# Attention probabilities: VectorE divides both heads of pair 1, GpSimd none of them

## The chip, the cores and the metric

The kernel runs on one core of a Trainium2 chip. Its five engines are TensorE (PE; its weight loads are shown apart as PEld), VectorE (DVE), ScalarE (ACT), GpSimd (POOL) and SyncE (SP), which issues the DMAs. The metric is the time of one execution on the device in microseconds, lower is better. Each engine runs its own program in order; they wait for each other on semaphores.

## What is computed

The reference takes x and a context of shape (4, 1024, 512) and does two things, all in fp32:

```python
x = x + banded_attention(layernorm(x), ctx, ctx)      # band of 128, one head of 512
x = x + two_layers(layernorm(x))
# each layer, HEADS = 8, DIM_HEAD = 64, WINDOW = 256:
q, k, v = split(shift_token(x) @ wqkv)
q, k = rotary_xpos(l2norm(q) * q_scale, l2norm(k) * k_scale)
sim = where(i < j or i > j + 256, -big, 8 * q @ k.T)
x = x + (softmax(sim) @ v) @ wo
h = layernorm(shift_token(x)) @ w1 + b1
a, g = split(h)
x = x + (a * gelu(g)) @ w2 + b2
```

What matters here is softmax(sim) @ v of the two layers: exponentials, their sums, and the division by the sums before the product with v.

## The kernel before

The 4096 rows are 32 tiles of 128. The program is a banded stage, then for each of two layers an attention stage (attend) and an FFN stage (ffn). Products in fp32 precision are made from a high and a low half of each operand: ScalarE makes the high half by a rounding copy (copy, L1363), VectorE the low half by a subtraction (low, L1727), and TensorE multiplies three combinations.

In attend(l), step s works on tile t = s - 2 for scores and probabilities while it projects tile s and rotates tile s - 1. k = t % 8 is the place of a tile in its sequence; it sees 1, 2 or 3 key tiles (k = 0, 1, from 2 on), so rows of probabilities are 128, 256 or 384 columns wide. The eight heads are four pairs; a pair's probabilities stand in one buffer lprob of 128 x 2 x 384. Each step has two halves, d = 0 for pairs 0 and 1, d = 1 for pairs 2 and 3. For a half of a tile:

- TensorE: scores(t, d) (L1094), two pairs after each other. Before its second pair it waits for hT_low, the low half of the transposed input: of tile s at d = 0, of tile s + 1 at d = 1. In this step VectorE makes the half of tile s + 1, in hT (split_h).
- VectorE: maximum(t, h) for the four heads of the half (L1893; it adds the mask, writes the exponents to lprob and gives the least value; a small read of an accumulator follows).
- ScalarE: probabilities (L1542), the exponentials with their sums.
- VectorE: divide(t, p) takes the reciprocals of a pair's two sums (L1878) and multiplies. Pair 0 is done whole by VectorE with one tensor_tensor (L1883). Of pairs 1, 2 and 3 (LATE_PAIRS) VectorE does the second head with a tensor_scalar (L1881) and GpSimd the first with another (divide in pool_program, L2295).
- TensorE: turn_probabilities (L1116) half a step later, pair 1 before pair 0; it waits for the maxima of the whole tile (lmax), since it writes the banks of the scores, and for each head's division (wait_scaled). ScalarE copies the result (lprobT), and mix (L1133) multiplies it with v.

VectorE's order at d = 0 is: four maxima, rope(.., 0) (with_cos and with_sin, L1917), norm_sum (L1825), divide(t, 0), divide(t, 1), rope(.., 1), split_h, then split_parts (even t, 2 to 22) or split_sums (odd t, 1 to 21), low halves of FFN weights that are prepared on the side. At d = 1 it begins with the next four maxima and split_out, divides pairs 2 and 3, and ends with split_q and split_k.

GpSimd's order in a step is: in some steps sums of weight parts (sum_parts), rotate(.., 0) (L2304), inverse_norm (a clamp, L2221, and a power function, L2222), divide(t, 1), scale_rotated(.., 0) (L2315), rotate(.., 1), scale_rotated(.., 1), divide(t, 2), divide(t, 3). What scale_rotated leaves in turned_qk is transposed by TensorE in turn_q and turn_k (L897) at the end of the step. The order on every engine is written out by hand in the loops over s.

Of the kernel before, what the change touches and what calls it, by code (L numbers as in the profile page):

```python
# [60 lines left out]
def hid_rows(j):  # L61
    return min(P, HID - j * P)
# [63 lines left out]
def reach(t):  # L126
    k = t % TPB
    w = min(k, 2) + 1
    return k, w, w * P, (k - w + 1) * P
# [5 lines left out]


PAIRS = HEADS // 2
LATE_PAIRS = (1, 2, 3)


PARTS = (2, 0, 1)
# [33 lines left out]
def early_tile(s):  # L175

    i, odd = divmod(s - NORMALISE_AT, 2)
    return i if 0 <= i < GROUP and not odd else None


def prepared_item(s, after):

    item, odd = divmod(s - PREPARE_AT - after, 2)
    return item if 0 <= item < HC and not odd else None


def summed_rows(s, after):

    pair = s - PREPARE_AT - 2 * HC - after
    return pair if pair in (0, 1) else None  # L190
# [24 lines left out]
def build(nc, x, ctx, mask, wqkv, q_scale, k_scale, wo, ln_g, ln_b, w1, b1, w2, b2, consts, out):  # L215
# [266 lines left out]
    def rotated_tile(s):  # L482

        return 0 if s == 0 else s - 1 if 2 <= s <= TILES else None

    def rotated_by_gpsimd(l, t, part):

        return 4 * (l * TILES + t) + 2 * (part + 1) - 2 * (l + ((t, part) > (0, 0)))
# [403 lines left out]
    def tensor_program(e):  # L892
# [146 lines left out]
        def attend(l):  # L1039
# [59 lines left out]
            def wait_scaled(n, p, i):  # L1099
                if p not in LATE_PAIRS:  # L1100
                    w.wait_ge(S("pscaled"), PAIRS * n + p + 1)
                elif i:
                    w.wait_ge(S("pscaled"), PAIRS * n + p + 1)
                else:
                    w.wait_ge(S("pscaled_pool"), len(LATE_PAIRS) * n + LATE_PAIRS.index(p) + 1)

# [610 lines left out]
    def vector_program(e):  # L1717
# [145 lines left out]
        def attend(l):  # L1863
# [8 lines left out]
            def divide(t, p):  # L1872
# [6 lines left out]
                w.wait_ge(S("rden"), PAIRS * n + p + 1)  # L1879
                if p in LATE_PAIRS:  # L1880
                    ins = e.tensor_scalar(prob[:, 1, 0:cols], prob[:, 1, 0:cols], inverse[:, 1:2], None, ALU.mult)  # L1881
# [280 lines left out]
    def pool_program(e):  # L2162
# [3 lines left out]
        def settle(ins):  # L2166

            ins.then_inc(S("pool_settled"), 1)
            w.wait_ge(S("pool_settled"), next(settled))
# [40 lines left out]
        def scale_tables(l):  # L2210
            A = attends[l]
            w.wait_ge(S("rope_in"), 64 * (l + 1))
            spread = A.scales[:, :].unsqueeze(1).to_broadcast([P, TPB, 2 * HD])
            for table in (A.rope_cos, A.rope_sin):
                e.tensor_tensor(table[:, :, :], table[:, :, :], spread, ALU.mult).then_inc(S("rope_scaled"), 1)

        def inverse_norm(l, t):
            n = l * TILES + t
            nm = norm[:, n % 2, :]
            w.wait_ge(S("norm_sum"), n + 1)  # L2220
            settle(e.tensor_scalar(nm[:, 0:16], nm[:, 0:16], NORM_FLOOR ** 2, 0.0, ALU.max, ALU.add))  # L2221
            e.tensor_tensor(nm[:, 16:32], nm[:, 0:16], half_power[:, :], ALU.pow).then_inc(S("norm_inverse"), 1)  # L2222
# [31 lines left out]
        def attend(l):  # L2254
            A, base = attends[l], l * TILES

            def wait_phase():

                if l:
                    w.wait_ge(S("down"), GROUP * GROUPS * HC * l)  # L2260
                    w.wait_ge(S("f_out"), base)
                else:
                    w.wait_ge(S("mix"), TILES)
                    w.wait_ge(S("x1"), TILES)

            def combine(op, to, a, b):
                return e.tensor_tensor(to, a, b, op)

            def sum_parts(j):

                n = 2 * hid_rows(j)
                g1, a1, a2, g2 = (raw_sum[:, i * n:(i + 1) * n] for i in range(4))
                s1, s2, s3, s4 = (part_sum[:, i * n:(i + 1) * n] for i in range(4))
                w.wait_ge(S("parts_in"), 48 * (l * (HC + 2) + j + 1))
                settle(combine(ALU.add, s1, g1, g2))
                combine(ALU.subtract, s3, a1, g1)
                settle(combine(ALU.subtract, s2, s1, a1))
                combine(ALU.subtract, s4, a2, s2).then_inc(S("part_sums"), 1)

            def sum_first_rows(pair):  # L2280

                odd1, even1, even2, odd2 = (raw_sum[:, i * HALF:(i + 1) * HALF] for i in range(4))
                t1, t2, t3, t4 = (part_sum[:, i * HALF:(i + 1) * HALF] for i in range(4))
                w.wait_ge(S("parts_in"), 48 * (l * (HC + 2) + HC + pair + 1))
                settle(combine(ALU.subtract, t1, odd1, even1))
                combine(ALU.subtract, t3, odd2, odd1)
                settle(combine(ALU.subtract, t2, odd2, t1))
                combine(ALU.subtract, t4, even2, t2).then_inc(S("part_sums"), 1)

            def divide(t, p):  # L2290

                n, cols, sm = base + t, reach(t)[2], small[:, (base + t) % 2, :]
                prob = A.prob[p][:, 0, 0:cols]
                w.wait_ge(S("rden"), PAIRS * n + p + 1)
                e.tensor_scalar(prob, prob, sm[:, 16 + 2 * p:17 + 2 * p], None, ALU.mult).then_inc(S("pscaled_pool"), 1)  # L2295

            def rotate(t, part):
                n, h2 = base + t, HD // 2
                turned, cos, sin = (by_head(x[:, part, :]) for x in (A.turned_qk, A.with_cos, A.with_sin))
                w.wait_ge(S("with_cos"), 2 * n + part + 1)  # L2300
                w.wait_ge(S("with_sin"), 2 * n + part + 1)
                w.wait_ge(S("k_turned") if part else S("q_turned"), n)
                for a, b in ((0, h2), (h2, 0)):
                    e.tensor_tensor(turned[:, :, a:a + h2], cos[:, :, a:a + h2], sin[:, :, b:b + h2],  # L2304
                                    ALU.add).then_inc(S("rotated"), 1)

            def scale_rotated(t, part):
                n = base + t
                turned = by_head(A.turned_qk[:, part, :])
                inverse = norm[:, n % 2, 16 + part * HEADS:16 + (part + 1) * HEADS]  # L2310
                w.wait_ge(S("rotated"), rotated_by_gpsimd(l, t, part))
                if part and t == 0:
                    w.wait_ge(S("first_rotated"), 2 * (l + 1))
                w.wait_ge(S("norm_inverse"), n + 1)
                e.tensor_tensor(turned, turned, inverse.unsqueeze(2).to_broadcast([P, HEADS, HD]),  # L2315
                                ALU.mult).then_inc(S("qk_scaled"), 1)

            if l:
                scale_tables(l)
            wait_phase()  # L2320
            for s in range(TILES + 3):
                t = s - 2
                live, rotating = 0 <= t < TILES, rotated_tile(s)
                if l and s == 0:
                    inverse_norm(l, 0)
                if prepared_item(s, 1) is not None:
                    sum_parts(prepared_item(s, 1))
                if summed_rows(s, 1) is not None:
                    sum_first_rows(summed_rows(s, 1))
                if s == 2:  # L2330
                    inverse_norm(l, 1)
                if rotating is not None:
                    rotate(rotating, 0)
                if rotating and s > 2:
                    inverse_norm(l, rotating)
                if live:
                    divide(t, 1)
                if rotating is not None:
                    scale_rotated(rotating, 0)
                    if rotating:  # L2340
                        rotate(rotating, 1)
                    scale_rotated(rotating, 1)
                if early_tile(s) is not None:
                    inverse_deviation(l, early_tile(s))
                if live:
                    divide(t, 2)
                    divide(t, 3)

        def inverse_deviation(l, t):
            reciprocal_deviation(stats[:, t % 2, :], "ln", l * TILES + t).then_inc(S("ln_rstd"), 1)  # L2350
# [40 lines left out]
        for l in range(DEPTH):  # L2391
            attend(l)
            ffn(l)
# [58 lines left out]
```

## Time and profile before

| | |
|---|---|
| time, median of 3 runs | 2882.64 us (2881.0 to 2884.29) |
| time of the profiled execution | 2882.62 us |
| its span | 2880.8 us |
| busy: PE, PEld | 2863.6, 2521.9 us |
| busy: DVE, ACT, POOL | 2069.0, 1346.0, 1308.8 us |
| TensorE's granted clock | 1.00 |

The busy times are of the whole span and average over stages with different limits. The ends of matmuls are modelled, so a gap of TensorE that is short can show as a longer group of matmuls, or as a gap between two weight loads, and not as idle time. In a window, the columns are its ends and length, then for PE, PEld, DVE, ACT and POOL the busy us (and instructions), then the granted clock, the DMA engines' share and GB/s. In the timeline a row is start, duration, engine, line, operation, output<-inputs, shapes and count of instructions merged; in brackets the idle time before it and what ended it. Instructions of one engine overlap by some 0.08 us from row to row. A power function of GpSimd works on 16 columns only.

### The profile page before, as it was taken

To read this page: it belongs to the slowest core of one execution; us is meant where nothing else is said; L and a number is where in the kernel's file an instruction comes from. 1 tells how busy PE (TensorE), PEld (TensorE's weight loads), DVE (VectorE), ACT (ScalarE), POOL (GpSimd) and SP (SyncE) were. 2 spreads that over 40 slices of the span, in tenths; PEclk is the share of its full clock that TensorE was granted. 3 is DMA by queue.
4 is the path that set the end of the run, shared out by engine and by line. 5 is a ranking of instruction groups with operands and counts; after the bars stand their busy time and mean duration, and the time that the engine had idled before them with its cause. 6 is when DMAs were issued, how large, how long until landed. Compare 5 with 4: busy or idle time off the path is not lost. (4 is left out here: it accounts for less than half of the span.)

```text
span 2880.8 us, 53016 instructions
## 1 busy us (share of the span) xinstructions
PE 2863.6 (99%) x20256; PEld 2521.9 (88%) x20256; DVE 2069.0 (72%) x4135; ACT 1346.0 (47%) x2807; POOL 1308.8 (45%) x1406
## 2 busy tenths in 40 slices
PE   9999999999999999999999999999999999999999
PEld 7887888888889999999998888888888999999998
DVE  8987677776677666766657777776677776676765
ACT  7875556565564222222235566655555322223221
POOL 7857676776641211122105676776662223222221
PEclk9999999999999999999999999999999999999999
DMA  6753233322047777777783223332127777777775
GB/s 218 237 187 109 94 109 103 121 92 81 30 178 299 271 273 265 269 265 258 262 312 120 96 94 108 111 118 90 51 66 294 278 276 272 274 288 281 282 268 195
DMA packets 184897, 547.02 MB, mean 190 GB/s; under 512 B 26678, under 2 KB 82490, under 8 KB 162116
## 3 DMA queue, kind: packets, MB, share of 16 engines
q1 hardware_dynamic: 184500, 543.57, 53.0%
q8 instruction: 161, 2.64, 0.4%
q14 instruction: 92, 0.75, 0.1%
q10 hardware_dynamic: 144, 0.07, 0.0%
HBM read 447.11 MB, written 93.70 MB: 188 GB/s over the span
## 5 line engine op out<-in xcount | busy, mean ns | idle before, releaser
L1251 PE MATMUL quad<-fhT_f,slot_f 128*128 128x256 f32 (+1 forms) x2088 | 594.6, 285 | 0.0
L1252 PE MATMUL quad<-fhT_f,slot_f 128*128 128x256 f32 (+1 forms) x2088 | 590.0, 283 | 0.0
L1253 PE MATMUL quad<-fhT_f,slot_f 128*128 128x256 f32 (+1 forms) x2088 | 589.9, 283 | 0.0
L1253 PEld LDWEIGHTS quad<-fhT_f,slot_f 128*128 128x128 f32 (+1 forms) x2088 | 392.7, 188 | 0.0
L1252 PEld LDWEIGHTS quad<-fhT_f,slot_f 128*128 128x128 f32 (+1 forms) x2088 | 392.7, 188 | 0.0
L1251 PEld LDWEIGHTS quad<-fhT_f,slot_f 128*128 128x128 f32 (+1 forms) x2088 | 392.5, 188 | 0.0
L1674 ACT ACTIVATE gate_f_raw<-gate_f_raw,bias_f 128x512 f32<-128x512 f32 (+1 forms) x176 | 127.2, 723 | 551.1 <-DVE gate_f_raw L2097 551.1
L1542 ACT ACTIVATE lprob<-lprob,small 128x384 f32<-128x384 f32 (+2 forms) x512 | 288.7, 566 | 138.5 <-DVE small L1893 138.5
L2187 POOL TENSOR_SCALAR stats<-stats 128x1 f32<-128x1 f32 x64 | 35.4, 553 | 690.1 <-DVE stats L2037 689.3
L2304 POOL TENSOR_TENSOR turned_qk<-with_cos,with_sin 128x256 f32<-128x256 f32 x252 | 183.1, 747 | 334.3 <-DVE with_sin L1917 242.4
L1000 PE MATMUL bank_pair<-wqkv_h,hT 128*128 128x512 f32 x992 | 323.6, 407 | 0.0
L1893 DVE CUSTOM_DVE_ANT_0 lprob<-quad,far 128x384 f32<-128x384 f32 (+2 forms) x512 | 229.2, 503 | 99.5 <-PE quad L1094 99.2
L2295 POOL TENSOR_SCALAR lprob<-lprob,small 128x384 f32<-128x384 f32 (+2 forms) x192 | 226.4, 1186 | 18.4 <-DVE small L1878 18.4
L1363 ACT ACTIVATE lprobT<-quad 128x768 f32<-128x768 f32 (+2 forms) x256 | 173.1, 728 | 103.2 <-PE quad L1116 103.0
L2363 POOL TENSOR_TENSOR res_f<-res_f,bias_f 128x512 f32<-128x512 f32 x63 | 87.8, 1394 | 283.0 <-DMA res_f<-stream 283.0
L2108 DVE SCALAR_TENSOR_TENSOR u_f<-sums_f,bias_f,gate_f_raw 128x512 f32<-128x512 f32 (+1 forms) x176 | 148.1, 841 | 93.3 <-ACT gate_f_raw L1674 93.3
L1000 PE MATMUL bank_pair<-wqkv_l,hT 128*128 128x512 f32 x496 | 201.7, 407 | 0.0
L2222 POOL TENSOR_TENSOR norm<-norm,half_power 128x16 f32<-128x16 f32 x64 | 195.9, 3061 | 5.3
L1000 PEld LDWEIGHTS bank_pair<-wqkv_h,hT 128*128 128x128 f32 x992 | 173.3, 189 | 25.5
L1727 DVE TENSOR_TENSOR qT<-quad,qT 128x512 fp32r<-128x512 f32 x64 | 44.3, 691 | 203.5 <-ACT qT L1363 203.5
L1133 PEld LDWEIGHTS bank<-lprobT,v_rows 128*64 128x64 f32 x2688 | 144.1, 137 | 45.3 <-issue 42.0
L2097 DVE TENSOR_TENSOR gate_f_raw<-quad,sums_f 128x512 f32<-128x512 f32 (+1 forms) x174 | 120.3, 691 | 79.9 <-PE quad L1253 77.1
(296 smaller groups left out, 7469.1 us busy)
## 6 DMA issues: line engine op xcount, KB each, us to landing
slot_f<-parts SPq DMA_DIRECT2D x160, 1792.0 KB, 7.5
slot_f<-parts SPq DMA_DIRECT2D x16, 1190.0 KB, 5.2
s_in<-stream SPq DMA_DIRECT2D x128, 128.0 KB, 2.8
s_res<-stream SPq DMA_DIRECT2D x64, 256.0 KB, 2.9
stream<-a_out SPq DMA_DIRECT2D x64, 256.0 KB, 2.0
res_f<-stream SPq DMA_DIRECT2D x63, 256.0 KB, 7.2
h_in_f<-stream SPq DMA_DIRECT2D x112, 128.0 KB, 6.7
parts<-part_high SPq DMA_DIRECT2D x20, 512.0 KB, 2.6
```

The lines of the kernel that those rows point to most:

```text
L1000: ins = e.matmul(bank, A.hT[n % 2][:, i % 2, c * P:(c + 1) * P], (wqkv_l if i == 2 else wqkv_h)[:, c, cols], start=(c, i) == (0, 0), stop= ...
L1133: ins = e.matmul(banks[5][half, p * P:(p + 1) * P], A.v_rows[:, k - tiles + 1 + j, h * HD:(h + 1) * HD], A.probT[p % 2][:, i, j * P:(j + 1 ...
L1251: e.matmul(bank[0:n, :], high, row_high, start=c == 0, stop=False)
L1252: e.matmul(bank[0:n, :], high, row_low, start=False, stop=False)
L1253: ins = e.matmul(bank[0:n, :], low, row_high, start=False, stop=c == 1)
L1363: return e.activation(to, source, ACT.Copy)
L1542: e.activation(prob, prob, ACT.Exp, bias=sm[:, h:h + 1], scale=-1.0, accum_out=sm[:, 8 + h:9 + h]).then_inc(S("lprob"), 1)
L1893: e.tensor_tensor_reduce(A.prob[h // 2][:, h % 2, 0:cols], quad[:, pair_banks(h // 2) + h % 2, 0:cols], A.far[:, WIN - cols:], 1.0, BIG, A ...
L2108: e.scalar_tensor_tensor(out=Fm.u[q % 2][0:n, :], in0=flat(Fm.sums[q % 2][0:n, 0:2, :]), scalar=Fm.bias1[0:n, 0, j:j + 1], in1=Fm.gate[q % ...
L2222: e.tensor_tensor(nm[:, 16:32], nm[:, 0:16], half_power[:, :], ALU.pow).then_inc(S("norm_inverse"), 1)
L2295: e.tensor_scalar(prob, prob, sm[:, 16 + 2 * p:17 + 2 * p], None, ALU.mult).then_inc(S("pscaled_pool"), 1)
L2304: e.tensor_tensor(turned[:, :, a:a + h2], cos[:, :, a:a + h2], sin[:, :, b:b + h2], ALU.add).then_inc(S("rotated"), 1)
```

## The change

The tuple of pairs that are divided by both engines loses pair 1, and GpSimd's call for it goes:

```diff
-LATE_PAIRS = (1, 2, 3)
+LATE_PAIRS = (2, 3)
@@ pool_program, attend @@
                 if rotating and s > 2:
                     inverse_norm(l, rotating)
-                if live:
-                    divide(t, 1)
                 if rotating is not None:
                     scale_rotated(rotating, 0)
```

The tuple is read in two more places. In VectorE's divide, pair 1 now takes the branch of pair 0: one tensor_tensor over both heads, with the two reciprocals as a broadcast operand. In TensorE's wait_scaled, both heads of pair 1 wait for pscaled, VectorE's count, and the count of GpSimd, pscaled_pool, goes up by two a tile, not three. No other instruction is added, removed or moved.

## Rows read from the trace of the kernel before

**Rows 1.** The page: busy time, then one window; columns as under the table above

```profile
PE 2863.6 (99%) x20256; PEld 2521.9 (88%) x20256; DVE 2069.0 (72%) x4135; ACT 1346.0 (47%) x2807; POOL 1308.8 (45%) x1406
...
250.00:800.00 550.00, 550.00 (x4050) 451.76 (x4049) 401.31 (x971) 325.99 (x736) 376.38 (x357) 1.00 0.27 91
```

**Rows 2.** Groups by line and form, VectorE, then GpSimd: count | busy us, mean ns

```profile
L1883 DVE TENSOR_TENSOR lprob<-lprob,small 128x768 f32<-128x768 f32 x48 | 54.4, 1133 | 1.7
L1883 DVE TENSOR_TENSOR lprob<-lprob,small 128x512 f32<-128x512 f32 x8 | 7.0, 880 | 0.3
...
L2295 POOL TENSOR_SCALAR lprob<-lprob,small 128x384 f32<-128x384 f32 x144 | 187.6, 1310 | 18.4 <-DVE small L1878 18.4
```

**Rows 3.** Whole run, waits of TensorE and its weight loads: us, times, longest

```profile
PE quad L897 <- POOL turned_qk L2315: 1.8, 3, 0.6
PE quad L1116 <- DVE small L1893: 0.5, 2, 0.2
...
PEld quad L1094 <- DVE hT L1727: 0.5, 2, 0.2
```

**Rows 4.** Timeline, tile 0 of layer 0 (k = 0): start us, duration us, engine, line

```profile
224.27 2.93 POOL L2222 TENSOR_TENSOR norm<-norm,half_power 128x16 f32<-128x16 f32 x1
225.12 0.42 DVE L1883 TENSOR_TENSOR lprob<-lprob,small 128x256 f32<-128x256 f32 x1
225.66 0.29 DVE L1881 TENSOR_SCALAR lprob<-lprob,small 128x128 f32<-128x128 f32 x1
...
227.79 0.41 PEld L1094 LDWEIGHTS quad<-kT,qT 64*128 64x128 f32 x6 [0.23 <-DVE hT L1727]
```

**Rows 5.** Timeline, tile 9 of layer 0 (k = 1): TensorE and VectorE

```profile
395.12 0.98 PE L1094 MATMUL quad<-kT,qT 64*128 64x256 f32 x12
...
400.67 0.35 DVE L1881 TENSOR_SCALAR lprob<-lprob,small 128x256 f32<-128x256 f32 x1
...
402.13 0.68 DVE L1727 TENSOR_TENSOR hT<-quad,hT 128x512 fp32r<-128x512 f32 x1
...
402.33 1.16 PE L1094 MATMUL quad<-kT,qT 64*128 64x256 f32 x12
```

**Rows 6.** Timeline, tile 10 of layer 0 (k = 2)

```profile
419.36 0.42 DVE L1881 TENSOR_SCALAR lprob<-lprob,small 128x384 f32<-128x384 f32 x1
419.48 3.09 POOL L2222 TENSOR_TENSOR norm<-norm,half_power 128x16 f32<-128x16 f32 x1
...
420.89 0.68 DVE L1727 TENSOR_TENSOR hT<-quad,hT 128x512 fp32r<-128x512 f32 x1
...
421.68 0.19 PEld L1094 LDWEIGHTS quad<-kT,qT 64*128 64x128 f32 x2
```

**Rows 7.** Timeline, tile 13 of layer 0 (k = 5)

```profile
482.47 0.69 DVE L1727 TENSOR_TENSOR hT<-quad,hT 128x512 fp32r<-128x512 f32 x1
...
484.11 0.19 PEld L1094 LDWEIGHTS quad<-kT,qT 64*128 64x128 f32 x2
...
485.99 0.55 DVE L1893 CUSTOM_DVE_ANT_0 lprob<-quad,far 128x384 f32<-128x384 f32 x1
...
487.08 1.46 PEld L1116 LDWEIGHTS quad<-ident,lprob 128*128 128x128 f32 x12
...
487.31 1.47 PE L1116 MATMUL quad<-ident,lprob 128*128 128x128 f32 x12
```

**Rows 8.** Timeline, last two tiles of layer 0 (30 and 31)

```profile
821.78 1.25 POOL L2295 TENSOR_SCALAR lprob<-lprob,small 128x384 f32<-128x384 f32 x1
...
823.35 1.53 PE L1116 MATMUL quad<-ident,lprob 128*128 128x128 f32 x12 [0.23 <-DVE small L1893]
...
826.78 0.66 PE L897 MATMUL quad<-ident,turned_qk 128*128 128x128 f32 x4 [0.60 <-POOL turned_qk L2315]
...
833.72 0.96 DVE L1883 TENSOR_TENSOR lprob<-lprob,small 128x768 f32<-128x768 f32 x1
...
834.85 1.47 POOL L2295 TENSOR_SCALAR lprob<-lprob,small 128x384 f32<-128x384 f32 x1 [5.67 <-DVE small L1878]
```

## The prediction

> **What bounds the kernel now.** I read the page's busy times first, then windows over the stages, then the waits of TensorE, then the timeline tile by tile. TensorE is busy for 99% of the span, and in a window of 550 us inside the first attention stage for all of it, at full granted clock; VectorE is busy for 401 of its 550 us and GpSimd for 376 [rows 1]. So neither VectorE nor GpSimd is the bound there. TensorE runs a fixed list of work for each tile, and the others only have to be in time for each of its waits. The waits that the profile books to TensorE are few: 1.8 us in three places for GpSimd's rotated queries and keys, 0.5 us in two for a maximum, and 0.5 us of its weight loads for the hT halves [rows 3]. That sets the most that can be won: little over 2 us of 2883. The question is therefore not how much work moves, but whether VectorE, given more to do inside a tile, becomes late for a wait of TensorE.
>
> In a tile VectorE's order is: four maxima of the first scores, the rope of queries, the squared norm, the division of pair 0, the division of pair 1, the rope of keys, the low half of hT, in most tiles a low half of the FFN weights, then the four maxima of the second scores. From the division of pair 0 to the hT half it runs without a gap, except where k = 0. TensorE needs two things from that string: hT, before the second half of scores(t, 1) (the wait on hT_low at an odd pair), and the last maximum, before turn_probabilities(t, 0).
>
> **What the change costs VectorE.** It removes one tensor_scalar over one head and puts a tensor_tensor over both in its place, 64 times. The old one takes 0.29, 0.35 and 0.42 us at 128, 256 and 384 columns [rows 4 to 6]. For the new one there are two prices in the rows of pair 0. Where GpSimd is idle, or sits in its power function, 2x128 columns took 0.42 and 2x384 took 0.96 [rows 4, 8]; between these, 2x256 is (0.42 + 0.96)/2 = 0.69. Where GpSimd's own tensor work stands beside it, the means are 0.88 at 2x256 and 1.13 at 2x384 [rows 2], 0.19 and 0.17 more. Which holds for pair 1? Its slot begins at 419.36, and GpSimd enters the 3.09 us power function at 419.48 [rows 6]; that is the situation of tile 0, where the pair 0 division of 0.42 ran inside the power function [rows 4]. I take the lower price: 0.13 more at 128 columns, 0.34 at 256, 0.54 at 384. The upper one gives about 0.32, 0.53 and 0.72.
>
> **Where it reaches TensorE.**
> - k = 1 (8 tiles, 4 a layer). The hT half ends at 402.13 + 0.68 = 402.81, 0.48 after scores(9, 1) began. That group already takes 1.16 against 0.98 for the same twelve matmuls before it [rows 5]: it stands still for some 0.18 already, so the slack is nothing and all of the 0.34 arrives. 8 x 0.34 = 2.7 us.
> - k = 2 (8 tiles). hT ends at 420.89 + 0.68 = 421.57; the first weight load behind the wait is at 421.68 [rows 6]. A release takes about 0.05 (227.79 in [rows 4] follows an hT half that ended at 227.74), so 0.06 is left, say 0.05. 0.54 - 0.05 = 0.49 arrives. 8 x 0.49 = 3.9 us.
> - k = 0. In the first tile of a layer the loads already sat still 0.23 for hT [rows 4]: 2 x 0.13 = 0.3 us. In the later ones VectorE idles before hT, and the addition is hidden.
> - k = 3 to 7. hT ends at 483.16 and is wanted at 484.11 [rows 7]: 0.95 less 0.05 covers 0.54. The last maximum ends at 485.99 + 0.55 = 486.54, and the loads of the turning begin at 487.08 [rows 7]: 0.49 after the release. The addition passes that by 0.05, but the load runs 0.23 ahead of its matmul (487.31), which takes up the rest: nothing, at this price. At 0.72 the load would be 0.23 late, of which that lead takes up between none and all; the middle, 0.12, would come through in the 16 tiles with odd k from 3 on that also split weight sums. Tiles with even k have VectorE idle before those maxima.
> - Stalls add up. Between two tiles VectorE idles for a microsecond or more waiting for the queries' high half, so it is in time again for the next, and TensorE has no idle time left in which to make one good.
>
> **What GpSimd gives back.** It loses 64 divisions, 1.31 us for the wide ones [rows 2], some 75 to 80 us of its own time. TensorE sees only the ends. In tile 30 GpSimd divides pair 1 at 821.78 for 1.25 us ahead of scaling and rotating tile 31, and TensorE then stands 0.60 us for the keys at 826.78 [rows 8]. Without the division GpSimd is done about 0.7 us sooner (1.25 less the 0.54 by which its power function, queued behind the longer division for their common port, starts later). But TensorE also arrives later: at 823.35 it already waits 0.23 for a maximum [rows 8], so 0.54 goes straight in there. 0.54 - 0.60 = -0.06, twice: -0.1 us. The remaining wait on GpSimd stands before layer 1's first tile, where nothing has been divided yet. The FFN stages have none of these instructions.
>
> **Sum.** 2.7 + 3.9 + 0.3 - 0.1 = 6.8 us. The profiled execution took 2882.62 us around its span of 2880.8, the median of the three runs is 2882.64: the same. 2882.6 + 6.8 = 2889.4 us, 0.24% slower. A measurement of this kernel tells about 0.2%, 5.8 us, from no change, so the forecast lies just beyond that.
>
> **The port rule.** In tile 0 the 0.42 us division ran wholly inside GpSimd's 2.93 us power function, which reads and writes SBUF [rows 4]; it was not held. The Trainium skill ("SBUF — State Buffer", Who interferes with whom) says that a VectorE instruction with two SBUF inputs and a GpSimd instruction that reads SBUF exclude each other for the whole instruction, whoever starts first. By that rule the 0.42 us division would have waited for the function's end, and the new one would wait whenever GpSimd gets in first; the row speaks against it for this function.
>
> **Rivals.**
> - Contended price. If GpSimd's work does stand beside the new division, as beside pair 0 [rows 2]: 8 x 0.53 + 8 x 0.67 + 2 x 0.32 + 16 x 0.12 + 2 x (0.72 - 0.60) = 12.4 us, 2895.0. For it: the norm's small clamp has only just ended when the division starts. Against it: the tensor_scalar in that slot shows its short 0.42.
> - Not slower: the cover holds. One mechanism: the pair 0 division loses its 0.19, because GpSimd, now early, does its clamp elsewhere, and hT comes nearly as before. k = 1 then keeps 0.15 and k = 2 keeps 0.30: 8 x 0.15 + 8 x 0.30 = +3.6, 2886.2, no measurable change. Were also the rest covered, only GpSimd's two waits of 0.60 would go: 2881.4. It decides where VectorE's string up to hT grows by less than 0.3 us a tile. Against it: GpSimd's rotation waits for VectorE's rope itself, so it cannot come earlier.
> - Power function first. If GpSimd enters it before the division and holds the port throughout, the division waits up to 3.09 us [rows 6]: hT late by 0.54 + 3.09 - 0.05 = 3.6 at k = 2, and the maxima by 3.1 beyond their slack in the others. 60 x 3 = 180 us, 3063. The order (419.36 before 419.48) and [rows 4] speak against it. This is what the port rule would give once the order flips; the Trainium skill's page named above states that rule.
>
> **How the numbers follow.** Chances: the forecast 0.56, contended price 0.18, cover holds 0.23 (0.10 at 2886, 0.13 at 2881), power function first 0.03. The forecast's own spread is 2886.5 to 2892: 0.15 us either way in each of the 16 tiles with k = 1 and 2. A quarter of it lies below the bound. So slower 0.42 + 0.18 + 0.03 = 0.63; same 0.14 + 0.20 = 0.34; faster, if GpSimd's relief shortens VectorE's own operations as well, 0.03. The range leaves out the 3063, most of the 0.13 and the top of the contended case: 2883.5 to 2896.5.
>
> **What the profile of the changed kernel would show.** Right: L1883 x128, with pair 1's near 0.96, 0.69 and 0.42; L1881 x128; L2295 x128; weight loads of L1094 waiting for hT in some 18 places, about 7 us in all; the tiles with k = 1 and 2 longer by 0.3 and 0.5 us, the rest unchanged; the 0.60 at the ends of both attention stages gone. Wrong if pair 1's division takes 1.1 or more, if k = 3 to 7 grow, or if scores(t, 1) at k = 2 still runs in one piece.

## The result and the profile after

The changed kernel takes 2888.63 us (median of 11 runs, 2887.63 to 2889.64) against 2882.51 us for the kernel before (11 runs): 6.1 us more, a ratio of 1.0021 with a 95% interval of 1.0013 to 1.0029. The prediction was 2889.4 us, with a range of 2883.5 to 2896.5.

The page's busy line and the window of [rows 1], now of the kernel after:

```profile
PE 2866.8 (99%) x20256; PEld 2522.6 (87%) x20256; DVE 2095.2 (73%) x4135; ACT 1345.8 (47%) x2807; POOL 1261.7 (44%) x1342
...
250.00:800.00 550.00, 548.63 (x4033) 449.22 (x4032) 408.09 (x963) 323.62 (x729) 355.75 (x327) 1.00 0.27 91
```

VectorE has 7 us more to do in this window and GpSimd 21 less. TensorE, which had no idle time in it, now has 1.4 us that the profile shows. Groups by line and form, as [rows 2]:

```profile
L1883 DVE TENSOR_TENSOR lprob<-lprob,small 128x768 f32<-128x768 f32 x96 | 100.3, 1045 | 3.3
...
L1883 DVE TENSOR_TENSOR lprob<-lprob,small 128x512 f32<-128x512 f32 x16 | 12.6, 787 | 0.6
...
L2295 POOL TENSOR_SCALAR lprob<-lprob,small 128x384 f32<-128x384 f32 x96 | 123.8, 1299 | 22.3 <-DVE small L1878 22.3
...
L2222 POOL TENSOR_TENSOR norm<-norm,half_power 128x16 f32<-128x16 f32 x64 | 224.4, 3507 | 5.3
```

The new division of pair 1 is averaged with pair 0's: (2 x 1045 - 1133) is 957 ns at 2x384 columns, (2 x 787 - 880) is 694 ns at 2x256. Pair 1's own instances bear that out: 0.96 us from k = 2 on, 0.69 at k = 1, 0.43 at k = 0, and none of the 64 takes longer than that. GpSimd's power function, which took 3.06 us on average, takes 3.51. It begins 0.11 us after the division, and at k = 1 it grew from 3.02 to 3.37, from k = 2 on from 3.09 to 3.63: by 0.35 and 0.54, as much as the division did. Waits of TensorE, then of its weight loads, as [rows 3]:

```profile
PE quad L897 <- POOL turned_qk L2315: 0.6, 1, 0.6
...
PE quad L1116 <- DVE small L1893: 0.5, 2, 0.3
```

```profile
PEld quad L1094 <- DVE hT L1727: 8.2, 18, 0.5
```

The weight loads of the scores stood twice for hT, 0.5 us; now 18 times, 8.2 us. Eighteen is two first tiles, eight with k = 1 and eight with k = 2. Not all of that is new time: at k = 1 the gap in front of the load that waits for hT was 0.31 us from load to load before, of which the profile booked nothing as a wait (with hT early it is 0.20, see before_early_half). The new time is read from the starts of scores(t, 0) of one tile and the next. Tile 10 and 11 before, where 395.12 of [rows 5] is tile 9:

```profile
412.84 1.31 PE L1094 MATMUL quad<-kT,qT 64*128 64x384 f32 x12
...
432.74 1.32 PE L1094 MATMUL quad<-kT,qT 64*128 64x384 f32 x12
```

and tiles 9, 10, 11 after:

```profile
396.47 0.74 PE L1094 MATMUL quad<-kT,qT 64*128 64x256 f32 x8
...
414.53 0.79 PE L1094 MATMUL quad<-kT,qT 64*128 64x384 f32 x6
...
434.84 0.45 PE L1094 MATMUL quad<-kT,qT 64*128 64x384 f32 x2
```

Tile 9 (k = 1) took 412.84 - 395.12 = 17.72 and takes 414.53 - 396.47 = 18.06: 0.34 more. Tile 10 (k = 2) took 19.90 and takes 20.31: 0.41 more. The same subtraction for all tiles of both layers gives, in us per tile (mean over the tiles of that kind; an execution's DMA waits in the FFN stages are outside it):

| kernel | first tile | k = 1 | k = 2 | k = 3 to 7 | tile 30 | all tiles |
|---|---|---|---|---|---|---|
| after, over before | +0.14 | +0.34 | +0.41 | 0.00 | -0.11 | +6.0 |

Tile 30 of each layer is left out of the column k = 3 to 7 and has its own; the later tiles with k = 0 are 0.00. The 62 tiles sum to 6.0 of the 6.1 us between the medians. (The two profiled executions are 6.7 us apart; the rest lies outside the attention stages.) Two places of the chain, first tile 9, as [rows 5] and [rows 4] (VectorE's division, GpSimd's power function that starts behind it, the hT half, the load it releases):

```profile
402.02 0.69 DVE L1883 TENSOR_TENSOR lprob<-lprob,small 128x512 f32<-128x512 f32 x1
...
402.13 3.37 POOL L2222 TENSOR_TENSOR norm<-norm,half_power 128x16 f32<-128x16 f32 x1
...
403.82 0.68 DVE L1727 TENSOR_TENSOR hT<-quad,hT 128x512 fp32r<-128x512 f32 x1
...
404.56 0.41 PEld L1094 LDWEIGHTS quad<-kT,qT 64*128 64x128 f32 x6 [0.46 <-DVE hT L1727]
```

The hT half ends at 404.50, the load comes at 404.56. Tile 10, as [rows 6], with the same six loads in the kernel before as the first line:

```profile
421.68 0.53 PEld L1094 LDWEIGHTS quad<-kT,qT 64*128 64x128 f32 x6
```

```profile
421.05 0.96 DVE L1883 TENSOR_TENSOR lprob<-lprob,small 128x768 f32<-128x768 f32 x1
...
423.12 0.68 DVE L1727 TENSOR_TENSOR hT<-quad,hT 128x512 fp32r<-128x512 f32 x1
...
423.86 0.47 PEld L1094 LDWEIGHTS quad<-kT,qT 64*128 64x128 f32 x6 [0.47 <-DVE hT L1727]
```

Counted from the start of the tile, the first load went from 421.68 - 412.84 = 8.84 to 423.86 - 414.53 = 9.33, 0.49 later. But the six loads, which took 0.53 when none of them waited, take 0.47 behind the wait, so the last one is only some 0.42 late.

And tile 13, as [rows 7], where nothing is late:

```profile
485.05 0.68 DVE L1727 TENSOR_TENSOR hT<-quad,hT 128x512 fp32r<-128x512 f32 x1
...
485.65 1.22 DVE L1727 TENSOR_TENSOR part_low<-part_low_raw,part_high 128x1024 fp32r<-128x1024 f32 x1
...
488.21 0.56 DVE L1893 CUSTOM_DVE_ANT_0 lprob<-quad,far 128x384 f32<-128x384 f32 x1
...
489.19 1.46 PEld L1116 LDWEIGHTS quad<-ident,lprob 128*128 128x128 f32 x12
```

The last maximum ends at 488.77, 0.42 ahead of the loads; it was 0.54 before. So only 0.12 of the 0.54 arrived there. Most of the rest was absorbed in front of the FFN weight half, where VectorE waited for ScalarE in the kernel before:

```profile
483.41 1.22 DVE L1727 TENSOR_TENSOR part_low<-part_low_raw,part_high 128x1024 fp32r<-128x1024 f32 x1 [0.25 <-ACT part_high L1363]
```

The end of the first attention stage, as [rows 8]:

```profile
825.58 0.50 PE L901 MATMUL bank<-wo_h,oT 128*128 128x512 f32 x1 [0.41 <-DVE oT L1727]
...
827.48 1.53 PE L1116 MATMUL quad<-ident,lprob 128*128 128x128 f32 x12 [0.27 <-DVE small L1893]
...
828.55 1.04 POOL L2315 TENSOR_TENSOR turned_qk<-turned_qk,norm 128x512 f32<-128x512 f32 x1
...
829.72 1.04 PE L897 MATMUL quad<-ident,turned_qk 128*128 128x128 f32 x8
...
832.42 1.32 PE L1094 MATMUL quad<-kT,qT 64*128 64x384 f32 x12 [0.20 <-DVE kT L1727]
```

The 0.60 us wait for the rotated keys is gone: GpSimd has them at 829.59, and all eight transpositions of queries and keys run as one group from 829.72. The 0.54 us by which VectorE is late came in instead, and ahead of the maximum: TensorE stands 0.41 us at 825.58 for oT, a low half that VectorE makes in this tile ahead of the maxima, where it had no wait before. Being late itself from there on, it waits for the maximum at 827.48 hardly longer than it did (0.27 against 0.23).

### The profile page after: what moved, and what is told of

The parts are those of the page before. It is cut to its first block and busy times, and to the rows that moved or that the text cites. A ratio compares the mean times of both kernels' runs of the same rounds, so it can differ in the third digit from the quotient of the medians.

```text
span 2887.5 us, 52952 instructions
## 1 busy us (share of the span) xinstructions
PE 2866.8 (99%) x20256; PEld 2522.6 (87%) x20256; DVE 2095.2 (73%) x4135; ACT 1345.8 (47%) x2807; POOL 1261.7 (44%) x1342
## 5 line engine op out<-in xcount | busy, mean ns | idle before, releaser
L2222 POOL TENSOR_TENSOR norm<-norm,half_power 128x16 f32<-128x16 f32 x64 | 224.4, 3507 | 5.3
L1133 PE MATMUL bank<-lprobT,v_rows 128*64 128x128 f32 x2688 | 175.1, 277 | 0.6 <-ACT lprobT L1363 0.6
```

The costliest lines, as they stand in the source:

```text
L1133: ins = e.matmul(banks[5][half, p * P:(p + 1) * P], A.v_rows[:, k - tiles + 1 + j, h * HD:(h + 1) * HD], A.probT[p % 2][:, i, j * P:(j + 1 ...
```

## Experiments

Each is the changed kernel (or, where said, the kernel before) with the edit shown. All were timed in five rounds beside the kernel before, and the column of tiles is worked out from each kernel's own trace as above, against the kernel before.

| kernel | median us | before, same rounds | ratio (95%) | first tile | k = 1 | k = 2 | k = 3 to 7 | tile 30 |
|---|---|---|---|---|---|---|---|---|
| narrow_split | 2882.73 | 2882.82 | 1.0000 (0.9992 to 1.0009) | 0.01 | -0.01 | 0.00 | 0.00 | -0.12 |
| narrow_only | 2888.69 | 2882.82 | 1.0021 (1.0012 to 1.0030) | 0.14 | 0.31 | 0.42 | 0.00 | 0.00 |
| two_scalars | 2886.55 | 2882.82 | 1.0013 (1.0004 to 1.0022) | 0.20 | 0.23 | 0.21 | 0.00 | -0.33 |
| early_half | 2883.24 | 2882.82 | 1.0001 (0.9992 to 1.0010) | -0.30 | 0.03 | 0.11 | 0.00 | -0.12 |
| before_early_half | 2882.92 | 2882.74 | 0.9999 (0.9991 to 1.0008) | -0.25 | 0.04 | 0.00 | 0.00 | 0.01 |
| relief_only | 2881.66 | 2882.74 | 0.9995 (0.9986 to 1.0004) | 0.00 | -0.01 | 0.00 | 0.00 | -0.65 |
| dose1 | 2889.94 | 2882.74 | 1.0024 (1.0015 to 1.0033) | 0.14 | 0.31 | 0.41 | -0.01 | 0.28 |
| dose2 | 2903.02 | 2882.74 | 1.0070 (1.0058 to 1.0083) | 0.16 | 0.31 | 0.42 | 0.28 | 0.67 |
| both_orders | 2885.48 | 2883.05 | 1.0009 (1.0000 to 1.0017) | -0.28 | 0.37 | 0.00 | 0.00 | -0.12 |
| late_weights | 2892.87 | 2883.05 | 1.0034 (1.0022 to 1.0046) | 0.16 | 0.79 | 0.42 | 0.00 | -0.11 |
| both_orders_12 | 2881.58 | 2882.65 | 0.9996 (0.9987 to 1.0005) | -0.29 | -0.13 | 0.00 | see text | -0.12 |
| split_orders_12 | 2881.63 | 2882.65 | 0.9998 (0.9989 to 1.0007) | -0.26 | -0.13 | 0.00 | 0.00 | -0.10 |

**narrow_split and narrow_only: in which tiles does the loss arise?** One predicate decides, tile by tile, whether pair 1 is split as before (TensorE's wait for each head follows it); narrow_split has it true for k < 3, narrow_only for k >= 3.

```diff
+def shared_first(t):
+    return t % TPB < 3          # narrow_only: t % TPB >= 3
@@ VectorE's divide @@
-                if p in LATE_PAIRS:
+                if p in LATE_PAIRS or (p == 1 and shared_first(t)):
@@ GpSimd's loop, after inverse_norm @@
+                if live and shared_first(t):
+                    divide(t, 1)
```

> Changed kernel, but in tiles with k = 0, 1, 2 pair 1 is split as before (VectorE one head, GpSimd the other). Theory hT (the whole loss is VectorE's longer string arriving late for the hT wait in the first tile of a layer and in k = 1 and 2): 2882.5 less the 0.1 of the two ends, 2882.4 us, no weight load of scores standing for hT beyond the before kernel's two places. Rival load (VectorE's 0.54 and GpSimd's power function, now 0.5 us longer, cost a little in every tile): 40 of 64 tiles keep the change, so 40/64 of 6.1 us stay, 2886.3. Rival pair 1 (its probabilities come late for the turning): same 2886.3, with waits of L1116.

> The complement: the change in tiles with k = 0, 1, 2 alone, the old split from k = 3 on. Theory hT: the whole loss stays, 8 x 0.34 + 8 x 0.42 + 2 x 0.13 = 6.3 us, 2888.8 us; the 0.60 us wait for the rotated keys at the end of both attention stages (tiles 30, k = 6) is back. Rival load: 24/64 of 6.1, 2884.8.

40 of the 64 tiles with the change cost nothing, the 24 others cost all of it, and of these the six later tiles with k = 0 are 0.00 again. In narrow_split the weight loads of the scores are back at two waits for hT:

```profile
PEld quad L1102 <- DVE hT L1736: 0.5, 2, 0.3
```

The rival of a cost in every tile, by contention or by GpSimd's longer power function, falls: it wanted 2886.3 and 2884.8.

**two_scalars: is it the length of the division?**

```diff
+                elif p == 1:
+                    for i in (0, 1):
+                        ins = e.tensor_scalar(prob[:, i, 0:cols], prob[:, i, 0:cols], inverse[:, i:i + 1], None, ALU.mult)
```

> Changed kernel, but VectorE does pair 1's two heads as two tensor_scalar instead of one tensor_tensor. From start to start the tensor_scalar takes 0.20, 0.26 and 0.33 us at 128, 256, 384 columns, so the addition over the kernel before is 0.20, 0.26, 0.33 and not 0.20, 0.34, 0.55. Theory hT: k = 1 8 x 0.26, k = 2 8 x (0.33 - 0.13), first tiles 2 x 0.1, ends 2 x (0.33 - 0.60): 2.1 + 1.6 + 0.2 - 0.5 = 3.4 us, 2885.9 us. Rival pair 1 (what matters is that one engine does both heads): 2888.6.

Measured 3.7 us over the kernel before where 3.4 were expected. With the same head count on the same engine, but a shorter string, the loss shrinks to 0.23 and 0.21 us at k = 1 and 2. So it is VectorE's time and not who divides. (In the first tile it is the other way, 0.20 against 0.14: at 128 columns two tensor_scalar, 0.20 us for the first to the start of the next and 0.28 for the second, are longer than one tensor_tensor of 0.43.)

**early_half and before_early_half: is it the wait for hT?** VectorE does the same work in another order.

```diff
+def half_first(s):
+    return 2 <= s < TILES - 1 and (s == 2 or (s - 2) % TPB in (1, 2))
@@ VectorE's loop @@
                         rope(rotated_tile(s), 1, A.with_cos, A.rope_cos, "with_cos")
+                        if half_first(s):
+                            split_h(s + 1)
                         rope(rotated_tile(s), 1, A.with_sin, A.rope_sin, "with_sin")
...
-                    if d == 0 and 1 <= s < TILES - 1:
+                    if d == 0 and 1 <= s < TILES - 1 and not half_first(s):
                         split_h(s + 1)
```

> Changed kernel with one more edit: in the first tile of a layer and in k = 1 and 2, VectorE makes the hT half between the two rope products of the keys instead of after them. VectorE's work is the same, only hT is 0.5 to 0.6 us earlier. Theory hT: both the loss and the 0.18 us that k = 1 already lost before are gone: 8 x (0.34 + 0.18) + 8 x 0.42 + 2 x (0.13 + 0.23) = 8.2 less 0.5 for what stays in the first tiles, 2881.0 us. Rivals load and pair 1: nothing changes, 2888.6 us.

> Kernel before, with the hT half made between the two rope products of the keys in the first tile of a layer and in k = 1 and 2. Theory hT: the hidden stalls of 0.18 (k = 1, 8 times) and 0.23 (first tiles, twice) go, 2882.5 - 1.9 = 2880.6 us. Rival (those were no stalls, only the shape of the group of matmuls): 2882.5.

The first half of the theory holds: with hT early, 0.4 us over the kernel before is left of the 6.1, and the waits for hT are gone. The second half missed: 2881.0 and 2880.6 were expected, 2883.2 and 2882.9 came. The trace of early_half at tile 9 shows why (the hT half, the FFN weight half, the last maximum, the loads of the turning), and below it the row of its waits:

```profile
401.60 0.69 DVE L1731 TENSOR_TENSOR hT<-quad,hT 128x512 fp32r<-128x512 f32 x1
...
402.81 1.22 DVE L1731 TENSOR_TENSOR part_low<-part_low_raw,part_high 128x1024 fp32r<-128x1024 f32 x1
...
404.97 0.42 DVE L1897 CUSTOM_DVE_ANT_0 lprob<-quad,far 128x256 f32<-128x256 f32 x1
...
405.45 0.86 PEld L1120 LDWEIGHTS quad<-ident,lprob 128*128 128x128 f32 x8 [0.41 <-DVE small L1897]
```

```profile
PEld quad L1120 <- DVE small L1897: 6.5, 16, 0.7
```

VectorE has the same work, only in a new order, so the maxima come no earlier: the last ends at 405.39, the loads of the probabilities stand 0.41 us for it. That wait stood right behind the one for hT. In the kernel before the last maximum of tile 9 ends at 405.55 and its load comes at 405.62, 0.02 us of slack behind a release of 0.05:

```profile
405.13 0.42 DVE L1893 CUSTOM_DVE_ANT_0 lprob<-quad,far 128x256 f32<-128x256 f32 x1
...
405.62 0.14 PEld L1116 LDWEIGHTS quad<-ident,lprob 128*128 128x128 f32 x1
```

In the changed kernel the slack is 0.26, because TensorE has already lost its time to hT. So the wait took hT's place, in 16 places where before_early_half has 10 and the changed kernel 4. In before_early_half the new order also costs VectorE idle time, since the half of hT that ScalarE makes is not ready so early:

```profile
401.51 0.69 DVE L1731 TENSOR_TENSOR hT<-quad,hT 128x512 fp32r<-128x512 f32 x1 [0.40 <-ACT hT L1367]
```

With that, its last maximum comes 0.25 us later in the tile than in the kernel before, and what hT gave back is lost again.

**relief_only: what is GpSimd's relief worth?** On the kernel before, GpSimd's call is dropped and VectorE keeps its one head; head 2 stays undivided, and TensorE waits for that head's exponentials alone. So this leaves out a part of the computation.

```diff
-                if live:
-                    divide(t, 1)
```

> Kernel before without GpSimd's division of pair 1, and nothing in its place: head 2 stays undivided, so this leaves out part of the computation. Shows what GpSimd's relief is worth alone. My theory: only the two waits of 0.60 us for the rotated keys at the ends of the attention stages go, 2882.5 - 1.2 = 2881.3 us. Rival (GpSimd's share also slows VectorE through the common port in every tile): 64 x 0.05 or more, below 2879.

1.1 us faster in the medians, not beyond the interval; the tiles show where: 0.65 in tile 30 of each layer and nothing elsewhere. The waits of TensorE for GpSimd fell from three to one, the one ahead of layer 1's first tile:

```profile
PE quad L897 <- POOL turned_qk L2317: 0.6, 1, 0.6
```

**dose1 and dose2: how much cover is there from k = 3 on?**

```diff
+                    for _ in range(1 if p == 1 and t % TPB >= 3 else 0):      # dose2: 2
+                        settle(ins)
+                        ins = e.tensor_scalar(prob[:, 1, 0:cols], prob[:, 1, 0:cols], 1.0, None, ALU.mult)
```

> Changed kernel; in tiles with k = 3 to 7 VectorE multiplies one head of pair 1 by 1.0 once more, about 0.4 us. Measures the cover that is left there. In the changed kernel's trace at tile 13 the hT half ends 0.43 us (after a release of 0.05) ahead of the load that wants it, and the last maximum 0.37 ahead. Theory hT (there is cover left): 0 to 0.05 us a tile in 40 tiles, 2888.6 to 2890.6 us. Rival load (each added 0.4 us on VectorE costs in every tile): 40 x 0.3, 2900.

> As dose1, but twice, about 0.8 us more on VectorE in the tiles with k = 3 to 7. Theory hT: the cover is passed: hT 0.8 - 0.43 = 0.35 us late in 40 tiles, 14 us, about 2902 us. If it stays near 2889, the cover is larger than I read.

Each dose makes hT of tile 13 about 0.4 us later in its tile (end at 9.26, 9.66 and 10.04 us from its start with none, one and two). dose1 costs nothing in these tiles but 0.28 - (-0.11) = 0.4 in tile 30, where there is no cover. dose2 costs 0.29 in 34 of them; in tile 29 of each layer there is more cover, and it costs nothing. Waits of the weight loads of dose1, then of dose2, with the hT half and the load of its tile 13:

```profile
PEld quad L1094 <- DVE hT L1727: 8.4, 18, 0.5
```

```profile
PEld quad L1094 <- DVE hT L1727: 20.5, 52, 0.5
...
487.46 0.68 DVE L1727 TENSOR_TENSOR hT<-quad,hT 128x512 fp32r<-128x512 f32 x1
...
488.20 0.47 PEld L1094 LDWEIGHTS quad<-kT,qT 64*128 64x128 f32 x6 [0.35 <-DVE hT L1727]
```

The second dose makes hT of tile 13 end at 488.14, and the load follows at 488.20: the wait of k = 1 and 2 has been brought about in tiles that had none. 18 waits for hT with one dose, 52 with two.

**both_orders and late_weights: what takes hT's place?** The low halves of the FFN weights go behind the second maxima; both_orders has early_half's edit as well.

```diff
-                    if d == 0 and prepared_item(s, 2) is not None:
+                    if d and prepared_item(s, 2) is not None:      # now after split_out
                         split_parts(l, prepared_item(s, 2))
-                    if d == 0 and prepared_item(s, 1) is not None:
+                    if d and prepared_item(s, 1) is not None:
                         split_sums(l, prepared_item(s, 1))
```

> Changed kernel with VectorE's order changed twice: the hT half between the rope products of the keys (first tile, k = 1, 2) as in early_half, and the low halves of the FFN weights after the second four maxima instead of before them. In early_half the wait moved from hT to the last maximum, behind a weight half of 0.95 or 1.22 us. Theory two waits: with both out of the way the 0.18 us that k = 1 lost before is won as well, 8 x 0.18 + 2 x 0.3 + 2 x 0.12 = 2.2 us under the kernel before, 2880.5 us. Rival (0.18 was never a stall of TensorE's work): 2882 to 2883, as early_half.

> Changed kernel with only the second of the two edits: FFN weight halves after the maxima, hT in its old place. Theory two waits (in the changed kernel hT is the wait that ends last in the first tiles, k = 1 and k = 2, the maximum only behind it): no gain, 2888.6 us. Rival (the loss is the maximum, which VectorE reaches late): most of the 6 us gone, 2883.

Both came out slower than either theory had said. k = 2 behaved (0.00 with both edits, 0.42 with one), and two tiles show what was expected of both_orders: tile 1, ahead of the trouble, is 0.16 and tile 25, behind the last weight, 0.09 shorter than before. But tiles 9 and 17 are 0.79 and 0.85 longer, and in the second layer their like, 41 and 49, 0.39 and 1.42. The chain in both_orders at tile 9, GpSimd's rows and TensorE's:

```profile
397.79 1.55 POOL L2273 TENSOR_TENSOR part_low_raw<-raw_part_raw 128x256 f32<-128x256 f32 x2 [7.47 <-DMA raw_part_raw<-in_L_ffn_w]
...
403.35 2.93 POOL L2228 TENSOR_TENSOR norm<-norm,half_power 128x16 f32<-128x16 f32 x1
...
408.99 1.04 POOL L2321 TENSOR_TENSOR turned_qk<-turned_qk,norm 128x512 f32<-128x512 f32 x1
...
410.09 0.66 PE L901 MATMUL quad<-ident,turned_qk 128*128 128x128 f32 x4 [0.59 <-POOL turned_qk L2321]
```

The halves are stored by DMAs, and only then the next weights are loaded, for GpSimd to add up at the head of its step. Where the tile before is the short one, k = 0, the later round trip is not done in time: GpSimd stands 7.47 us for the load at 397.79, starts its power function at 403.35, has the rotated keys at 410.03, and TensorE waits 0.59 us for them.

That is tile 9 alone. In the other three TensorE waits for hT again, by two other ways. At tile 17 (and 49) the late stores hold up SyncE, which issues the DMAs in order, and with it the early store behind them (normed rows for the first FFN tiles, out of the buffer that ScalarE writes its squares to). It is issued 0.93 us before tile 17 begins, and in the changed kernel 3.45. ScalarE stands 3.32 us for that, VectorE's rope 1.05 for ScalarE, and TensorE 0.42 for hT:

```profile
557.56 1.03 ACT L1493 ACTIVATE square<-bank_pair 128x1024 f32<-128x1024 f32 x1 [3.32 <-DMA early<-square]
...
558.62 0.69 DVE L1921 TENSOR_TENSOR with_cos<-bank_pair,rope_cos 128x512 f32<-128x512 f32 x1 [1.05 <-ACT square L1493]
...
564.07 0.50 PE L1098 MATMUL quad<-kT,qT 64*128 64x256 f32 x4 [0.42 <-DVE hT L1731]
```

At tile 41 GpSimd is late with its rotation and so stands beside pair 1's division, which takes 1.03 us there and not 0.69 (GpSimd's row, then VectorE's):

```profile
1737.19 1.88 POOL L2310 TENSOR_TENSOR turned_qk<-with_cos,with_sin 128x256 f32<-128x256 f32 x2
...
1738.58 1.03 DVE L1887 TENSOR_TENSOR lprob<-lprob,small 128x512 f32<-128x512 f32 x1
```

That is the contended price of the prediction's first rival, here 0.34 above the free one at 2x256, where 0.19 had been reckoned. Tile 9 has it too (1.03), but hT, being early, bears it there. late_weights has all of this with hT in its old place, and its waits for hT grow, up to 0.95 to 1.02 us of TensorE in tiles 9, 17 and 49. In the tiles without the trouble it is as the changed kernel (k = 2 0.42, first tiles 0.16), so it decides only this much: the maximum was not the wait that ended last, since to relieve it gave nothing.

```profile
PEld quad L1094 <- DVE hT L1727: 10.5, 18, 1.2
```

**both_orders_12 and split_orders_12: both waits relieved where they bind.** The late weights only for k = 1 and 2; split_orders_12 also has narrow_split's division.

```diff
+def weights_at(s):
+    return 1 if (s - 2) % TPB in (1, 2) else 0
...
+            def split_weights(s):
+                if prepared_item(s, 2) is not None:
+                    split_parts(l, prepared_item(s, 2))
+                if prepared_item(s, 1) is not None:
+                    split_sums(l, prepared_item(s, 1))
@@ VectorE's loop, in both places @@
-                    if d == 0 and prepared_item(s, 2) is not None:
-                        split_parts(l, prepared_item(s, 2))
-                    if d == 0 and prepared_item(s, 1) is not None:
-                        split_sums(l, prepared_item(s, 1))
+                    if d == weights_at(s) == 0:
+                        split_weights(s)
...
+                    if d == weights_at(s) == 1:          # behind split_out
+                        split_weights(s)
```

> As both_orders, but the FFN weight halves go behind the maxima only in tiles with k = 1 and 2; elsewhere they stay. In both_orders every half was later, the DMAs of the next weights came later, and GpSimd, waiting for them ahead of tiles 9 and 17, was late with the rotated keys (0.59 us at 410.09). Theory two waits: without that, 8 x (-0.17) for k = 1, 0 for k = 2, 2 x (-0.3) for the first tiles, 2 x (-0.12) for the ends: -2.2 us against the kernel before, 2880.7 us, that is all 6.1 us of the loss undone and the older 0.18 too, with VectorE doing the same work as in the changed kernel. Rival (the DMA round trip is as tight in k = 1): 2884 or more.

> The same two orders, and pair 1 split between the engines in k = 0, 1, 2 as in narrow_split: a candidate for the fastest. Theory two waits: once hT and the maximum are in time the split no longer matters, 2880.7 us as both_orders_12. If the division's length in k = 1 and 2 still counts somewhere, this one is faster by it.

Both are 1.0 us under the kernel before and 7 under the changed one, 1.2 less than the sum said. k = 1 is 0.13 shorter than in the kernel before and k = 2 equal to it, with both kinds of division. In the profiled execution of both_orders_12 tile 11 is 1.53 us longer: ScalarE stood 5.76 us there for the early store, as in tile 17 of both_orders. In the other kernel it stood 4.39 us there, and tile 11 is 0.15 longer. How often that happens in the executions that were only timed is not known; it may be a part of the missing 1.2. Waits of split_orders_12:

```profile
PEld quad L1110 <- DVE hT L1744: 0.2, 1, 0.2
...
PEld quad L1133 <- DVE small L1910: 2.3, 5, 0.7
```

With both waits out of the way it does not matter who divides pair 1. Against the kernel before, 1.0 us is within the interval, so it is a tie, not a faster kernel.

## Why the prediction was right

- **The bound.** TensorE's list of work sets the tile, and the others matter only at its waits. relief_only and dose1 show it from both sides: 71 us less on GpSimd is worth 1.1 us, and 0.4 us more on VectorE in the tiles with k = 3 to 7 is worth nothing there, save in tile 30. The list of waits that it began with was not whole, though. The largest, four of kT, another low half of VectorE's, was left out. Two of them stand ahead of the second tile of each layer (1.1 us each) and two ahead of tile 30 of each layer (0.2 us each), and the division has no part in them:

```profile
PE quad L1094 <- DVE kT L1727: 2.6, 4, 1.1
```

- **The price of the division.** The lower one was taken, 0.54 and 0.34 us more than the tensor_scalar, because GpSimd is about to enter its power function then. The trace has 0.957 and 0.694 us for the new instruction (0.96 and 0.69 foretold). The contended price did not come here; it came in both_orders, when GpSimd had been made late.
- **k = 1.** 8 x 0.34 foretold, 8 x 0.34 measured; narrow_only and early_half show that the place is the hT wait. That a stall lay there already was right, its size of 0.18 was not quite: in the traces with hT early the load comes 0.10 to 0.11 us earlier, and with both waits relieved (both_orders_12) the eight tiles are 0.13 shorter. The term does not depend on it, since with no slack left all of the 0.34 arrives. That moving hT alone would win it, as expected of early_half, was wrong, since the maximum stood right behind.
- **k = 2.** 8 x 0.49 foretold, 8 x 0.41 measured. This is the term that was mis-sized, by 0.08. The load is delayed by 0.49 as worked out, but the six loads behind the wait then take 0.47 and not 0.53, and the delay of the last one, 0.42, is what the tile is longer.
- **First tiles and ends.** 2 x 0.13 and -2 x 0.06 foretold, 2 x 0.14 and -2 x 0.11 measured; the later tiles with k = 0 hide it, as said. The trade at the end is narrow_split's and relief_only's tile 30: 0.65 out at the keys (0.60 foretold), 0.54 in. The 0.54 came in at oT, 1.9 us ahead of the maximum that had been named.
- **k = 3 to 7.** Nothing, as said, but the reason for the maximum was only partly right, and in that the zero was in part luck. The step said that 0.54 would pass the 0.49 of slack by 0.05 and be caught by the lead of the load. In fact only 0.12 arrived, since VectorE had been waiting 0.25 us for ScalarE ahead of the weight half. That idle time was in the trace and not in the working. Whether the lead of a load can catch a delay was not put to the test in these tiles.

The sum of the measured terms is 2.7 + 3.3 + 0.3 - 0.2 = 6.1 us (6.0 before rounding), against 6.8. The forecast's own spread was added up a little too wide: 16 x 0.15 = 2.4 us gives 2887.0 at its lower end, not 2886.5.

## What to carry to other kernels

Where one engine is busy all the time, list the other engines' deadlines with it, tile kind by tile kind, and hold each addition against each deadline: the mean load of the helper (73%) said nothing here, and the 16 tiles with k = 1 and 2 carried 6.0 of the 6.1 us. A wait that is relieved uncovers the next one, a few tenths of a microsecond behind it or less, so both have to be read before a gain is promised. And work that is moved to where an engine idles moves what follows it too: the DMAs, whatever is queued behind them, and the moments at which two engines stand beside each other.

## What the runs showed that was not expected

GpSimd's power function of 16 columns went from 3.06 to 3.51 us on average with the division beside it, and it starts before the division has ended: 402.13 against 402.02 to 402.71 in tile 9. narrow_split has both divisions in one trace: at k = 2, behind a tensor_scalar of 0.42, the function takes 3.09, and at k = 3, behind the tensor_tensor of 0.96, 3.63. In the first tile of the kernel before, a division ran wholly inside it without being held, and the function took 2.93 [rows 4]. So the start of the function is held up by a division, and a division is not held up by the 3 us of the function. The Trainium skill ("SBUF — State Buffer", SBUF: two separate sides, and Who interferes with whom) has two such instructions exclude each other for their whole length; these rows agree with it only at the start. The runs show the durations, not what is locked.
